# A fused mLSTM-attention and expert-FFN block: gate products on four column groups, ScalarE's copies in another order, tiles on three banks

## The reference

```python
ig = gate_in @ igate_w.T + igate_b          # gate_in = [q, k, v], 8 gates each
fg = gate_in @ fgate_w.T + fgate_b
log_f = jax.nn.log_sigmoid(fg)
csum = jnp.cumsum(log_f, axis=-1)           # with a zero in front
log_D = tril(csum[t+1] - csum[s+1]) + ig[s]
D = jnp.exp(log_D - max_log_D)
qk = jnp.einsum('bhsd,bhtd->bhst', qh, k_scaled)
k_hop = jnp.einsum('bhvc,vmhc->bhvm', qh, rpe[hops])
C = (qk + k_hop) * D
normalizer = jnp.maximum(jnp.abs(jnp.sum(C, axis=-1, keepdims=True)), jnp.exp(-max_log_D))
h = (C / (normalizer + EPS)) @ vh           # then a layer norm per head, weight 1 + ln_w, bias ln_b
```

## Time and profile before

| | |
|---|---|
| median of three runs | 3395.26 us |
| the profiled execution | 3399.43 us, of which its span 3397.4 us |
| TensorE busy | 3031.3 us (89%) |
| VectorE busy | 2467.2 us (73%) |
| ScalarE busy | 1920.0 us (57%) |
| GpSimd busy | 2023.1 us (60%) |
| mean granted TensorE clock | 0.953 of 2.4 GHz |

### The profile page before, as it was taken

One profiled execution on the slowest core, in us unless ns is written; L12 is line 12 of the kernel. 1 busy time (PEld: TensorE's weight loads), 2 busy tenths in 40 slices (PEclk: granted clock), 3 DMA queues, 4 the chain that ended last, 5 costly groups with the idle time before them and its releaser, 6 DMA issues.

```text
span 3397.4 us, 69927 instructions
## 1 busy us (share of the span) xinstructions
PE 3031.3 (89%) x24660; PEld 1893.3 (56%) x24660; DVE 2467.2 (73%) x5132; ACT 1920.0 (57%) x4590; POOL 2023.1 (60%) x2195
## 2 busy tenths in 40 slices
PE   6778777787778876899999999999999999999997
PEld 4555545554445544556655666666565656566554
DVE  5655555555555555788888888888888888888875
ACT  3444444444444443666666666666666666666663
POOL 6777777777777775354554554545545545545453
PEclk8898898899999897899999999999999999999999
DMA  8999999999999998655555555555555555556541
GB/s 273 343 351 349 326 343 348 342 347 348 348 343 352 343 349 274 179 178 174 167 176 171 182 172 163 186 167 173 177 175 168 178 175 167 175 170 190 163 146 62
DMA packets 412814, 799.46 MB, mean 235 GB/s; under 512 B 107034, under 2 KB 211482, under 8 KB 410420
## 3 DMA queue, kind: packets, MB, share of 16 engines
q1 hardware_dynamic: 311476, 453.08, 42.6%
q0 software_dynamic: 82560, 270.60, 23.8%
q10 hardware_dynamic: 18432, 71.31, 5.4%
HBM read 618.02 MB, written 176.69 MB: 234 GB/s over the span
## 4 chain that ended last, share of the span: by engine, by line
PE 67%; DMA 13%; POOL 9%; issue 5%; DVE 4%; ACT 2%; SPq 0%; POOLq 0%; ACTq 0%; DVEq 0%
DMA arena<-in_L_xattn_rpe_dram,arena 13%; PE psum L1720 12%; PE psum L1641 9%; PE psum L1653 8%; PE psum L1671 8%; PE psum L1558 8%; POOL arena L772 6%; PE psum L1585 6%; PE psum L1574 5%; PE psum L1700 4%; PE psum L1724 3%; PE psum L1616 3%; POOL arena L759 2%; PE psum L1527 1%; ACT arena L941 1%
## 5 line engine op out<-in xcount | busy, mean ns | idle before, releaser
L772 POOL DMA_INDIRECT arena<-in_L_xattn_rpe_dram,arena x768 | 732.5, 954 | 239.9 <-issue 188.2
L1558 PE MATMUL psum<-arena 128*128 128x128 f32 x4128 | 629.5, 303 | 169.0 <-DMA arena<-in_L_xattn_rpe_dram,arena 156.5
L1558 PEld LDWEIGHTS psum<-arena 128*128 128x128 f32 x4128 | 503.8, 154 | 404.7 <-DMA arena<-in_L_xattn_rpe_dram,arena 262.3
L969 ACT ACTIVATE arena<-arena 128x512 f32<-128x512 f32 (+3 forms) x1024 | 496.7, 555 | 42.3 <-PE psum L1671 39.2
L1305 DVE TENSOR_TENSOR arena<-psum,arena 128x1024 f32<-128x1024 f32 (+1 forms) x384 | 387.0, 1043 | 150.0 <-PE psum L1653 144.8
L1720 PE MATMUL psum<-arena 128*128 128x512 f32 x1024 | 492.8, 595 | 3.0 <-DVE arena L1355 2.1
L568 DVE COPY arena<-psum 128x416 f32<-128x416 f32 (+15 forms) x512 | 225.4, 442 | 290.7 <-PE psum L1574 282.4
L559 DVE COPY arena<-psum 128x512 f32<-128x512 f32 x384 | 263.5, 688 | 231.7 <-PE psum L1558 228.1
L1574 PE MATMUL psum<-arena 64*32 64x416 f32 (+7 forms) x8192 | 368.9, 430 | 59.6 <-ACT arena L883 37.2
L797 POOL TENSOR_SCALAR_AFFINE_SELECT arena<-arena 128x256 f32<-128x256 f32 x256 | 124.2, 485 | 494.5 <-ACT arena L969 493.6
L559 ACT COPY arena<-psum 128x512 f32<-128x512 f32 x384 | 225.9, 589 | 242.0 <-PE psum L1558 238.5
(11 more groups left out here) (111 smaller groups left out, 4726.2 us busy)
## 6 DMA issues: line engine op xcount, KB each, us to landing
arena<-in_x_dram SPq DMA_DIRECT2D x256, 256.0 KB, 4.3
arena<-gate_rows SPq DMA_DIRECT2D x128, 512.0 KB, 4.6
arena<-in_x_dram SPq DMA_DIRECT2D x512, 64.0 KB
arena<-in_ctx_dram SPq DMA_DIRECT2D x32, 1024.0 KB, 7.4
out_dram<-arena SPq DMA_DIRECT2D x128, 256.0 KB, 2.1
arena<-in_L_xattn_rpe_dram,arena POOLq DMA_INDIRECT x1032, 6.5
arena<-hop_products SPq DMA_DIRECT2D x128, 128.0 KB, 2.6
arena<-hop_products SPq DMA_DIRECT2D x128, 120.0 KB, 2.5
```

The lines of the kernel that those rows point to most:

```text
L772: nc.gpsimd.indirect_dma_start(out=rows[set_of(n, v)][:, t, :], out_offset=None, in_=rpe[:, :], in_offset=bass.IndirectOffsetOnAxis(ap=her ...
L969: last = nc.scalar.activation(decay[u % DECAYS][:, e, at:at + width], top_pair[p % 2][:, e * S + j * P:e * S + j * P + width], ACT.Exp, bi ...
L1558: last = nc.tensor.transpose(turn_bank(o)[:, q * P:(q + 1) * P], own[:, q * P:(q + 1) * P], ident)
```

## The change

1. **Gate products.** The gate weights are laid out in 32 columns (GW = 32): rows 0 to 7 the forget gates, 8 to 15 the input gates, the rest zero. The eight products go to four column groups of one bank: the product of feature tile k lands in PSUM rows 32k to 32k+31, first the four of the queries, then the four of the context on top. So the four partial sums have to be added: ScalarE copies rows 64 to 127 (64 by 512), and VectorE adds in three operations ("two", "half", "zi"). The bank is now 4, not 6: `gates` waits for VectorE's sum of head pair 0, which frees bank 4, and the first `weigh` of pair 2 waits for the gates' readers. `base` of tile 0 no longer does.
2. **Forget gate.** ScalarE now makes the absolute value and the negated minimum (Abs, Relu) in `gate_log`, and exp and logarithm in `gate_softplus`. The subtraction (L1276 before) is taken into the sum over the tokens, which keeps the opposite sign. The input gates are moved to rows 32 to 39 by a small DMA (`move_igate`) on SyncE's queue, ahead of the context's load; `gates_3` waits for it.
3. **ScalarE's order.** `mix_turned(rf, 0)` stands ahead of `gate_log`, `ffn_turned(rf, 1)` ahead of `gate_softplus`, and `mix_turned(rf, 1)` ahead of `unit_decay(ra, 10)`.
4. **Banks of the second step.** Context tile 3 is turned first, into bank 7, then tile 2 into bank 5, query tile 0 into bank 6, query tile 1 into bank 7. Query tile 0 no longer waits for a copy of the same step. `weigh` of unit 3, the first in bank 5, waits for the copy of tile 2.
5. **Third step.** `turn_ffn(rf, 0)` stands ahead of the back turn of pair 0.

The helper that makes a turn, `turn(b, src)`, is unchanged: four transposes of 128 by 128. The diff, cut to what bears on this:

```diff
+    GW = P // KT
...
-        C_TURN, C_BANK = [0, 0, 1, 1], [4, 7, 6, 7]
+        C_TURN, C_BANK = [0, 0, 1, 1], [4, 7, 5, 7]
         X_TURN, X_BANK = [1, 1, 2, 2], [6, 7, 6, 6]
         MIX_AT = 2 * P
+        GATE_BANK = 4
...
+            def move_igate(r):
+
+                sp.wait_ge(dve_p.sem, dve_p.done(r.b, "zi"))
+                sp.dma_start(g_i, g_zi[NH:2 * NH, :]).then_inc(igate_moved, 16)
...
                 def gate_context():
                     act.wait_ge(pe_p.sem, pe_p.done(rp.b, "gates"))
                     act.wait_ge(dve_p.sem, dve_p.done(rp.b, "a", 1))
-                    nc.scalar.copy(g_ctx[0:GR, :], bank(6)[2 * FG:2 * FG + GR, :]).then_inc(
+                    nc.scalar.copy(g_ctx[0:2 * GW, :], bank(GATE_BANK)[2 * GW:4 * GW, :]).then_inc(
                         act_p.sem, act_p.step("gctx"))
                 def gate_log():
-                    act.wait_ge(dve_p.sem, dve_p.done(rp.b, "abs"))
+                    act.wait_ge(dve_p.sem, dve_p.done(rp.b, "zi"))
+                    nc.scalar.activation(g_l[0:NH, :], g_zi[0:NH, :], ACT.Abs).then_inc(
+                        act_p.sem, act_p.step("abs"))
+                    nc.scalar.activation(g_m[0:NH, :], g_zi[0:NH, :], ACT.Relu, scale=-1.0).then_inc(
+                        act_p.sem, act_p.step("relu"))
+
+                def gate_softplus():
...
+                if rf:
+                    mix_turned(rf, 0)
...
                 def gates_1():
                     dve.wait_ge(act_p.sem, act_p.done(rp.b, "gctx"))
-                    nc.vector.scalar_tensor_tensor(g_zi[0:GR, :], bank(6)[0:GR, :], g_b[0:GR, :], g_ctx[0:GR, :],
-                                                   ALU.add, ALU.add).then_inc(dve_p.sem, dve_p.step("zi"))
-                    dve.wait_ge(dve_p.sem, dve_p.done(rp.b, "zi"))
-                    nc.vector.scalar_tensor_tensor(g_l[0:NH, :], g_zi[FG:GR, :], -1.0, g_zi[FG:GR, :], ALU.mult,
-                                                   ALU.max).then_inc(dve_p.sem, dve_p.step("abs"))
-                    nc.vector.tensor_scalar(g_m[0:NH, :], g_zi[FG:GR, :], 0.0, None, ALU.min).then_inc(
-                        dve_p.sem, dve_p.step("min"))
+                    got = bank(GATE_BANK)
+                    nc.vector.tensor_tensor(got[GW:2 * GW, :], got[GW:2 * GW, :], g_ctx[GW:2 * GW, :],
+                                            ALU.add).then_inc(dve_p.sem, dve_p.step("two"))
+                    if rp.b:
+                        dve.wait_ge(igate_moved, rp.b * 16)
+                    nc.vector.scalar_tensor_tensor(g_zi[0:GW, :], got[0:GW, :], g_b[0:GW, :], g_ctx[0:GW, :],
+                                                   ALU.add, ALU.add).then_inc(dve_p.sem, dve_p.step("half"))
+                    dve.wait_ge(dve_p.sem, dve_p.done(rp.b, "half"))
+                    nc.vector.tensor_tensor(g_zi[0:GW, :], g_zi[0:GW, :], got[GW:2 * GW, :],
+                                            ALU.add).then_inc(dve_p.sem, dve_p.step("zi"))
                 def gates_2():
                     dve.wait_ge(act_p.sem, act_p.done(rp.b, "ln"))
-                    dve.wait_ge(dve_p.sem, dve_p.done(rp.b, "min"))
-                    nc.vector.tensor_tensor(g_m[0:NH, :], g_m[0:NH, :], g_l[0:NH, :], ALU.subtract).then_inc(
-                        dve_p.sem, dve_p.step("logf"))
-                    dve.wait_ge(dve_p.sem, dve_p.done(rp.b, "logf"))
                     dve.wait_ge(act_p.sem, act_p.done(rp.b, "floor", 1))
-                    nc.vector.tensor_tensor_scan(g_c[0:NH, :], one[0:NH, :].to_broadcast([NH, S]), g_m[0:NH, :], 0.0, ALU.mult,
+                    nc.vector.tensor_tensor_scan(g_c[0:NH, :], g_l[0:NH, :], g_m[0:NH, :], 0.0, ALU.add,
                                                  ALU.add).then_inc(dve_p.sem, dve_p.step("cum"))
                 def gates_3():
                     dve.wait_ge(dve_p.sem, dve_p.done(rp.b, "cum"))
                     dve.wait_ge(pe_p.sem, pe_p.done(rp.b, "stats", 1))
-                    nc.vector.tensor_tensor(g_rows[0:NH, :], g_zi[0:NH, :], g_c[0:NH, :], ALU.subtract).then_inc(
+                    dve.wait_ge(igate_moved, rp.b * 16 + 16)
+                    nc.vector.tensor_tensor(g_rows[0:NH, :], g_i, g_c[0:NH, :], ALU.add).then_inc(
                         dve_p.sem, dve_p.step("a"))
...
-                    nc.vector.tensor_tensor(g_c[0:NH, :], g_c[0:NH, :], g_z[0:NH, :], ALU.add).then_inc(
+                    nc.vector.tensor_tensor(g_c[0:NH, :], g_z[0:NH, :], g_c[0:NH, :], ALU.subtract).then_inc(
...
                     elif t == 2:
+                        if rf:
+                            pe.wait_ge(dve_o.sem, dve_o.done(rf.b, ("sum", 3)))
+                    else:
+                        pe.wait_ge(act_p.sem, act_p.done(rp.b, ("c", 1)))
+                    turn(C_BANK[t], context[:, t, :]).then_inc(pe_p.sem, pe_p.step(("c", t)))
+
+                def turn_queries(t):
+                    pe.wait_ge(dve_p.sem, dve_p.done(rp.b, ("norm", t)))
+                    if t == 0:
                         pe.wait_ge(act_p.sem, act_p.done(rp.b, "stats", 1))
                         if rg:
                             pe.wait_ge(*dve_f.at(rg.b, ("out", ST - 1)))
                     else:
-                        pe.wait_ge(act_p.sem, act_p.done(rp.b, ("c", 1)))
-                    turn(C_BANK[t], context[:, t, :]).then_inc(pe_p.sem, pe_p.step(("c", t)))
-
-                def turn_queries(t):
-                    pe.wait_ge(dve_p.sem, dve_p.done(rp.b, ("norm", t)))
-                    pe.wait_ge(act_p.sem, act_p.done(rp.b, (("c", 2), ("c", 3), ("x", 0), ("x", 2))[t]))
+                        pe.wait_ge(act_p.sem, act_p.done(rp.b, (("c", 3), ("x", 0), ("x", 2))[t - 1]))
                     turn(X_BANK[t], xq_norm[t % 2]).then_inc(pe_p.sem, pe_p.step(("x", t)))
                 def gates():
                     pe.wait_ge(act_p.sem, act_p.done(rp.b, ("x", ST - 1)))
-                    for k in range(KT):
-                        for lo, w, src in ((0, gate_qT, qT[rp.par]), (2 * FG, gate_cT, kT[rp.par])):
-                            last = nc.tensor.matmul(bank(6)[lo:lo + GR, :], w[:, k, :], src[:, k, :],
-                                                    start=(k == 0), stop=(k == KT - 1))
+                    if ra:
+                        pe.wait_ge(dve_o.sem, dve_o.done(ra.b, ("sum", 0)))
+                    for i, (w, src) in enumerate(((gate_qT, qT[rp.par]), (gate_cT, kT[rp.par]))):
+                        for k in range(KT):
+                            last = nc.tensor.matmul(bank(GATE_BANK)[k * GW:(k + 1) * GW, :], w[:, k, :],
+                                                    src[:, k, :], start=(i == 0), stop=(i == 1))
                     last.then_inc(pe_p.sem, pe_p.step("gates"))
                 def gate_stats():
...
                         pe.wait_ge(pool_p.sem, pool_p.done(ra.b, ("center", ST - 1)))
                         if rp:
                             pe.wait_ge(act_p.sem, act_p.done(rp.b, ("c", 0)))
+                    if u == 3 and rp:
+                        pe.wait_ge(act_p.sem, act_p.done(rp.b, ("c", 2)))
                     if k == 0:
                         pe.wait_ge(dve_o.sem, dve_o.done(ra.b, ("sum", (p - 2) % 4), 1 if p < 2 else 0))
+                        if p == 2 and rp:
+                            pe.wait_ge(act_p.sem, act_p.done(rp.b, "gctx"))
+                            pe.wait_ge(dve_p.sem, dve_p.done(rp.b, "zi"))
                     pe.wait_ge(dve_a.sem, dve_a.done(ra.b, ("mul", u)))
...
                         if t == 2 and rp:
                             pe.wait_ge(act_p.sem, act_p.done(rp.b, "stats"))
                     elif rp:
-                        pe.wait_ge(act_p.sem, act_p.done(rp.b, "gctx"))
-                        pe.wait_ge(dve_p.sem, dve_p.done(rp.b, "zi"))
+                        pe.wait_ge(act_p.sem, act_p.done(rp.b, ("x", ST - 1)))
                     elif rg:
                         pe.wait_ge(*dve_f.at(rg.b, ("out", ST - 1)))
                     for k in range(KT):
...
                     if rp and d == 1:
+                        turn_context(3)
                         turn_context(2)
-                        turn_context(3)
                         turn_queries(0)
                         turn_queries(1)
                     if rp and d == 2:
                         turn_queries(2)
+                    if rf and d == 2:
+                        turn_ffn(rf, 0)
                     if ra and d in BACK:
                         turn_back(ra, BACK[d])
-                    if d == 2:
-                        if rf:
-                            turn_ffn(rf, 0)
-                        if rp:
-                            turn_queries(3)
+                    if rp and d == 2:
+                        turn_queries(3)
                     if rf and d >= 3:
                         base(rf, d - 3)
                     if rf and d >= 2:
```

47 lines of the change are left out of this document (27 added, 20 removed).

## The result

The changed kernel takes 3361.47 us (median of 4 runs, 3359.15 to 3364.62) against 3394.96 us for the kernel before (4 runs, 3393.3 to 3408.54): a ratio of 0.9897, 95% interval 0.9872 to 0.9922. It is faster, but by half of what I forecast (3329 us), and it lies outside my range of 3310 to 3358. The profiled execution took 3363.58 us with a span of 3361.5 us, 35.9 us less than the span before.

The account below looks back on a forecast made before the run. TensorE was taken to bound the kernel; its 2.33 us a round, limited by VectorE's mix, became 2.1: 29 × 2.1 + 3 × 1.6 = 66 us off 3399.4, 3333 profiled, 3329 forecast; own range 3320 to 3340, wider range 3310 to 3358.

Parts of the forecast that it names:

- Gate products: TensorE's eight gate products: on four column groups busy 1.95 us instead of 3.61, 1.66 us less; 1.60 a round taken.
- the change of shape in front of them: Before the gate products: the tiling shape now changes after 64-column products, a wait of at most 0.17 us.
- Three banks and the third step: TensorE's turns and routes: waits gone or shortened, 0.44 + 0.41 − 0.07 = 0.78 us a round gained.
- The wait on the pair sum: At gates: a new wait for VectorE's sum of head pair 0, no slack, 0.05 us.
- VectorE's operations: Gate chain on VectorE: 3380 ns removed, 2099 ns added by three new operations, 1.28 us a round less.
- In all VectorE comes 1.38 us earlier to the mix of tile 1: VectorE's chain up to that mix: 1.28 us less work plus 0.1 us of earlier start.
- The slack: Before turn_mix of tile 1: 0.74 us free in a mean round, so TensorE can gain 2.12 us there.
- The waits behind it: TensorE's later waits: 0.21 us at turn_mix, 0.1 for varying rounds; routes covered by 0.3 us.
- VectorE binds harder: Rival at VectorE's mix: new operations cost 0.92 us each, VectorE saves only 0.63; 3349 us, chance 0.17.
- Four groups are no faster: Rival at the gate products: they stay at 3.54 us, 0.73 us a round left; 3374 us, chance 0.07.
- slower: Rival: three new VectorE operations at 1.85 us each make routes wait 3.1 us; 3418 us, chance 0.03.
- ScalarE's order, priced at 0.1 us: ScalarE's queue: copying the mix ahead of the gate chain removes waits worth 0.1 us a round.

Follow-up runs that it names:

- e4: Changed kernel with each feature tile's query and context gate products issued back to back in the same column group: 3354.46 us, one execution.
- e8: e2 with the second step's tiles on two banks as before, tile 2 in bank 6: 3341.12 us, one execution.
- e9: Changed kernel, the router's guard reading one operand (maximum with 1e-30) and writing to PSUM: 3344.40 us, ratio 0.9823.
- e7: e2, with ScalarE copying FFN tile 1 ahead of Abs and Relu and gate_stats moved behind scores: 3319.43 us, ratio 0.9782.
- e10: e7 with e9's one-operand guard: 3307.30 us, ratio 0.9712.
- e2: Changed kernel with SyncE's load of residual tile 2 issued ahead of the sixteen hop-product loads of pair 3: 3329.74 us, ratio 0.9773.
- e6: Kernel before with half of the gate products left out (gates wrong), gates still in bank 6: 3393.43 us, ratio 0.9991.
- e11: e6 with the gates and their readers in bank 4: 3405.73 us, ratio 1.0002.
- e12: e2 with ScalarE's old order, Abs, Relu, exp and logarithm ahead of the mix copy of tile 0: 3460.33 us, one execution.
- e1: Changed kernel with the router's guard, still two SBUF operands, writing its result to bank 7 in PSUM: 3359.70 us, ratio 0.9854.
- e5: Kernel before with residual tile 2 loaded ahead of the hop products of pair 3: 3405.07 us against 3396.52, ratio 1.0023.

## Why the prediction was wrong

- **Gate products: right.** I took 1.66 us less from the hop stage's 64-by-32 products; it is 1.69. That four groups run at once with full rows too, and in either order, is shown by the trace after and by e4. For the change of shape in front of them I took 0.06 us from a bound of 0.17. The step grew by 0.20, but the wait for the pair sum is in it. The Trainium skill's "TensorEngine Tiling (Array Packing)", Key Properties, says that a change of mode drains TensorE; no run here shows what that costs at this place.
- **Three banks and the third step: right.** Forecast 0.78 us, measured 0.80; e8 brings the old wait back.
- **The wait on the pair sum: right that there is no slack, a little low in size.** I had 0.05 us for it and 0.06 for the shape, 0.11 together, and 0.20 were measured. The sum releases the gates in every round; in e8 the wait reaches 1.0 us.
- **VectorE's operations: right.** 2.10 us forecast for the three new ones, 2.12 measured, and one that writes PSUM in place is no dearer. But VectorE's busy time fell by 20 us (2467.2 to 2447.4), not by about 40, because the guard took more; ScalarE's rose by 25, not 40.
- **"In all VectorE comes 1.38 us earlier to the mix of tile 1": this step failed.** It came 0.63 us earlier. I added up what VectorE has to do and took everything else on it to keep its time. Up to the guard of tile 1 that nearly held: VectorE was 1.23 us earlier there. Then the guard itself took 0.89 us where it had taken 0.29, and 0.60 of the missing 0.75 us went. I had read the 1.28 us of L1386 as a slow case against a mean of 0.42, but that mean mixes four tiles: before, the guard of tile 0 took about 1.09 us on average, that of tile 1 0.29, those of tiles 2 and 3 0.16. A product of GpSimd ran beside the first two of them in every round. e9 shows the price: with a guard that does not stall, the mix comes 0.75 us earlier and the round is 0.48 us shorter. e7 and e10, which differ by the guard alone, show 0.30. That the guard of tile 1 would stall in 19 rounds of 28 and not in 3 could not be read from the rows, and its cause stays open.
- **What held VectorE besides.** `layer` of tile 2 waits for GpSimd, and GpSimd for a load whose issue stands behind 16 others. I had read the row of GpSimd's product for the tile before, and took it as a limit for the start of the chain but not for its middle. This wait took little more than before (0.38 to 0.44 us a round), so it is not where the forecast gain went. But it is a limit on any further gain: in e9 the time saved at tile 0's guard ended in it. Its removal in e2 is worth 0.94 us a round together with the guard's fewer stalls; about half of what the mix gains there is the guard's.
- **The slack.** I took 0.74 us of free time ahead of `turn_mix` in a mean round. Over 26 rounds of the kernel before, by the same working, the mean is 0.63.
- **The waits behind it.** For all new waits I had 0.36 us a round (0.21 at the mix, 0.05, 0.1 for rounds that vary); they are 1.40 without the pair sum's: 0.96 at the mix and 0.44 at `routes`, `base` and `gate_stats`. For `routes` of tile 1 I had 0.3 us of cover over ScalarE's copy behind Abs and Relu, and 0.13 us are lost. For `gate_stats` I had nothing. In e7 both are gone.
- **The rivals.** "VectorE binds harder" had the right place, TensorE waiting on the mix, but the wrong cause: it needed the new operations at 0.92 us each, and they took 0.71. Its 3349 us was still 12 us too low. "Four groups are no faster" and "slower" are refuted by the records of 128*32 and by the ratio.
- **Parts that I priced one by one.** My sum treats them as independent. They are not: the gate saving alone is worth nothing in the old order and bank (e6, e11), and ScalarE's order, priced at 0.1 us, is what keeps 4.4 us from coming back (e12). My sum held nonetheless for TensorE's work, as the change moves them together.

## What to carry to other kernels

When an engine gets rid of work, follow its chain up to the next point where another engine waits for it, and ask at each wait in between whether what it waits for moves as well; here a load behind sixteen others in its queue did not. A small operation that is slow in one round of a trace is not an outlier to be averaged away: count it in all rounds, place by place, and look at what runs beside it. If another engine's operation starts with it in every round and it stalls in only a few, its time can change with an edit that has nothing to do with it. Before a saving on the bounding engine is counted, look up who holds the bank it frees and in which order its readers stand, as the saving can turn whole into their wait.

## What the runs showed of the hardware

- Eight products of 128 rows by 32 columns over 512 columns, on four column groups, take 1.854 us start to start, against 3.541 for the same eight at 128 by 40 on two halves. The order within the groups makes next to no difference (1.878 in e4).
- A VectorE operation of one value a row with two SBUF inputs took up to 1.29 us beside GpSimd's 128 by 512 product, and ended with it. When it started 0.13 to 0.3 us behind the product it stalled every time; when both started within 10 ns it stalled in 3 of 28 rounds (before), 19 (after), 22 (e1) and 4 (e2), and took 0.16 us in the others. With one SBUF input and the output in PSUM it took 0.16 us in all rounds of e9 and e10. With one input in PSUM and one in SBUF the 32 by 512 additions took 0.68 to 0.74 us. A `tensor_scalar` from SBUF to SBUF, 8 by 512, has one input and still went from 1049 ns to 1479 on average when GpSimd's chain was moved beside it (e5).
- After TensorE had stood for 3.2 us, its granted clock was 0.50 for the 2.6 us that follow, and its products took twice their time there (e12); after the waits of up to 1.3 us in the kernel after it stayed at 1.00 in the full rounds.
